# Down projection of the shared experts and the attention's four projections: from float32 matmuls to three single passes of rounded parts and remainders

## The reference

```python
x = x + 0.5 * ffn(layernorm(x))
x = x + attention(layernorm(x))
x = x + 0.5 * ffn(layernorm(x))

def ffn(x):                     # 4096 tokens
    shared = (silu(x @ shared_gate.T) * (x @ shared_up.T)) @ shared_down.T     # 256 -> 512 -> 256
    top_id = argmax(x @ gate_w.T); xs = x * sigmoid(max(x @ gate_w.T))         # 8 experts
    routed = swiglu of xs with the weights of expert top_id                    # 256 -> 512 -> 256
    return shared + routed

def attention(x):               # 16 heads of 16 features, 64 landmarks
    k, q, v = split_heads(x @ Wk), split_heads(x @ Wq) / 4, split_heads(x @ Wv)
    q_l, k_l = means of q and k over each 8 tokens
    s1, s2, s3 = softmax(q k_l'), softmax(q_l k_l'), softmax(q_l k')
    z = pinv(s2)                # 6 iterations, each four 64x64 products in a chain
    return (s1 @ (z @ (s3 @ v))) @ Wo + bo
```

## Time and profile before

| | us |
|---|---|
| median of 3 runs | 1280.99 (1280.19 to 1283.07) |
| the profiled execution | 1283.79 |
| its span, first to last instruction | 1281.9 |
| PE busy | 1176.8 (92%) |
| DVE busy | 708.9 (55%) |
| ACT busy | 559.7 (44%) |
| POOL busy | 539.8 (42%) |

### The profile page before, as it was taken

One profiled execution on the slowest core, in us unless ns is written; L12 is line 12 of the kernel. 1 busy time (PEld: TensorE's weight loads), 2 busy tenths in 40 slices (PEclk: granted clock), 3 DMA queues, 4 the chain that ended last, 5 costly groups with the idle time before them and its releaser, 6 DMA issues.

```text
span 1281.9 us, 28898 instructions
## 1 busy us (share of the span) xinstructions
PE 1176.8 (92%) x10692; PEld 923.2 (72%) x10693; DVE 708.9 (55%) x1387; ACT 559.7 (44%) x887; POOL 539.8 (42%) x603
## 2 busy tenths in 40 slices
PE   4899999999995789999999999986899998999997
PEld 2688877888884456667676676764688887888886
DVE  7533236776663464656757557553642235666664
ACT  2422126666662445445354453421522224666663
POOL 0388205677773122322313231220168503766675
PEclk9899999999998799999999999997799999999999
DMA  8311523222111200000000000000611513222220
GB/s 327 149 50 50 193 77 108 64 68 74 59 61 53 83 2 3 2 3 2 3 2 2 2 2 2 3 2 1 269 44 50 188 37 115 64 65 63 68 70 21
DMA packets 41953, 80.16 MB, mean 63 GB/s; under 512 B 8948, under 2 KB 33655, under 8 KB 40832
## 3 DMA queue, kind: packets, MB, share of 16 engines
q1 hardware_dynamic: 28576, 53.54, 11.5%
q0 software_dynamic: 13280, 25.24, 6.5%
HBM read 57.17 MB, written 27.07 MB: 66 GB/s over the span
## 4 chain that ended last, share of the span: by engine, by line
PE 82%; DVE 11%; issue 4%; ACT 2%; DMA 1%; DVEq 0%; POOL 0%; POOLq 0%; ACTq 0%
PE PS L1396 17%; PE PS L1346 13%; PE PS L1410 10%; PE PS L1355 9%; PE PS L1576 4%; PE PS L1469 4%; PE PS L1589 4%; PE PS L1626 3%; PE PS L1403 3%; PE PS L1477 3%; DVE A_NM L653 2%; DVE A_NM L660 1%; PE PS L1385 1%; PE PS L1536 1%; PE PS L1511 1%
## 5 line engine op out<-in xcount | busy, mean ns | idle before, releaser
L1396 PE MATMUL PS<-WHL,XGH 128*128 128x512 f32 x624 | 217.9, 431 | 8.2 <-DVE XGL L566 4.5
L1228 POOL TENSOR_TENSOR A_A<-A_XC,A_ST 128x320 f32<-128x320 f32 (+1 forms) x96 | 72.9, 774 | 234.3 <-ACT A_ST L1020 234.2
L1410 PE MATMUL PS<-WD,XNT 128*128 x624 | 148.5, 381 | 1.5 <-ACT XNT L956 1.5
L1158 POOL DMA_INDIRECT X<-xs_dram,WHO x78 | 115.0, 1475 | 46.9 <-issue 46.9
L1396 PEld LDWEIGHTS PS<-WHL,XGH 128*128 128x128 f32 x624 | 111.7, 191 | 30.6 <-issue 7.9
L919 ACT ACTIVATE HSB<-PS 128x512 f32<-128x512 f32 x64 | 38.2, 597 | 216.3 <-PE PS L1346 216.3
L1164 POOL DMA_INDIRECT HSB<-shared_dram,WHO x78 | 81.1, 1040 | 114.7 <-DMA shared_dram<-X 91.4
L573 DVE TENSOR_TENSOR XNT<-XNT,PS 128x512 f32<-128x512 f32 x78 | 53.7, 688 | 135.0 <-PE PS L1396 135.0
L514 DVE TENSOR_TENSOR HB<-HSB,PS 128x512 f32<-128x512 f32 x64 | 44.0, 688 | 151.8 <-ACT HSB L919 151.8
L1396 PE MATMUL PS<-WHL,XGL 128*128 128x512 f32 x312 | 124.2, 398 | 0.0
L1410 PEld LDWEIGHTS PS<-WD,XNT 128*128 128x128 f32 x624 | 112.4, 190 | 14.5 <-issue 2.0
(11 more groups left out here) (205 smaller groups left out, 2323.4 us busy)
## 6 DMA issues: line engine op xcount, KB each, us to landing
WG<-in_r_gate SPq DMA_DIRECT2D x2, 4096.0 KB, 15.6
WU<-in_r_up SPq DMA_DIRECT2D x2, 4096.0 KB, 18.0
xs_dram<-X SPq DMA_DIRECT2D x16, 512.0 KB, 2.9
WD<-in_r_down SPq DMA_DIRECT2D x4, 2048.0 KB, 8.3
shared_dram<-X SPq DMA_DIRECT2D x16, 512.0 KB, 8.0
X<-in_x SPq DMA_DIRECT2D x4, 1024.0 KB, 9.2
X<-mid_dram SPq DMA_DIRECT2D x8, 512.0 KB, 3.8
X<-xs_dram,WHO POOLq DMA_INDIRECT x78, 3.4
```

Source lines behind the costliest of these rows:

```text
L1158: pool.indirect_dma_start(out=B["XS"][:, u * D:(u + 1) * D], out_offset=None, in_=xs_dram, in_offset=bass.IndirectOffsetOnAxis(ap=B["WHO"] ...
L1228: pool.tensor_tensor(a, x, st, ALU.add).then_inc(att["a"], 1)
L1396: ins = pe.matmul(banks[bank][:], tok, w[:, k * F:(k + 1) * F], start=(k == 0 and i == 0), stop=(k == KD - 1 and i == 2))
L1410: ins = pe.matmul(banks[7][:, 0:D], B["HT"][:, u * F + f * P:u * F + (f + 1) * P], B["WD"][:, bass.ds(ex * (KF * D) + f * D, D)], start=(f ...
```

## The change

- Shared down projection: SDN is replaced by SDH (rounded, cast by ACT) and SDL (remainder, subtracted by POOL), both float32r. The raw weights are loaded into a free part of WU. SP's load of r_up waits for three splits instead of two.
- The product of the hidden part stays in HSB; ACT copies it to a rounded buffer HHL, DVE subtracts that from it for the remainder. HHL shares HB's memory and has two pairs of buffers.
- PE does three single passes (rounded x rounded, rounded x remainder, remainder x rounded) per token tile and f. Its order is now gate_up n, down n-2 throughout, across group borders. The addition to X (`shared_out`) of group g-1 moves behind f = 1 of group g. The groups are unrolled in all engines.
- Attention: ACT and POOL split WQ, WK, WV and WO at its start. Of the transposed tokens ACT makes the rounded part XTH, DVE the remainder XTL from the same bank (`low_tokens`, two calls per period, after `denominators` and after `s2_shift`). Of the outputs OT, ACT makes OTH after `sums_kept(nxt,1)`, POOL OTL between chain_a 4 and 5. All four projections become three single passes; PE's waits on `xts` become waits on `xtl`.
- Some buffers move (V, NUM onto the raw weights; TT, WS, BSEL into X's spare part), and six semaphores that only DVE waits for become one (`own`).

```diff
-            def shared_group(g, u, first=False, last=False):
+            def shared_out(g):
+                need(dve, "dn", g * KF + KF)
+                need(dve, "xs", g * GT + GT)
+                for jj in range(2):
+                    xg = X[:, g * GT * D + jj * 2 * D:g * GT * D + (jj + 1) * 2 * D]
+                    dve.scalar_tensor_tensor(xg, banks[7 if jj == 0 else 2][:], 0.5, xg, ALU.mult, ALU.add).then_inc(s["x_new"], 1)
+
+            def shared_group(g):
                 for f in range(KF):
+                    hidden = B["HSB"][:, (f % 2) * F:(f % 2 + 1) * F]
                     need(dve, "silu", g * KF + f + 1)
...
+                    dve.tensor_tensor(hidden, hidden, banks[5 + f % 2][:], ALU.mult).then_inc(s["h"], 1)
+                    need(dve, "hh", g * KF + f + 1)
+                    dve.tensor_tensor(B["HHL"][2 * (f % 2) + 1][:], hidden, B["HHL"][2 * (f % 2)][:].bitcast(F32), ALU.subtract).then_inc(s["hl"], 1)
+                    if f == 1 and g > 0:
+                        shared_out(g - 1)
+                    if f == 2 and g < NG - 1:
+                        low_tokens(g + 1, (g + 1) % 2)
...
+            def low_tokens(b, k):
+                dve.wait_ge(att["xth"], count("xth", b, k + 1))
+                part = slice(k * GW, (k + 1) * GW)
+                dve.tensor_tensor(B["XTL"][b % 2][:, part], banks[7 - k][:], B["XTH"][b % 2][:, part].bitcast(F32), ALU.subtract).then_inc(att["xtl"], 1)
...
                 if exists(old):
                     denominators(old)
+                if exists(far):
+                    low_tokens(far, 0)
                 if exists(nxt):
                     s2_shift(nxt)
+                if exists(far):
+                    low_tokens(far, 1)
                 if exists(done):
                     project(done, 0)
...
-                        for high, w in ((SGH, SG), (SUH, SU)):
+                        for high, w in ((SGH, SG), (SUH, SU), (SDH, SD)):
                             act.copy(high[:], w).then_inc(s_split_hi, 1)
...
+                    need(act, "h", g * KF + f + 1)
+                    if g * KF + f >= 2:
+                        need(act, "dn", g * KF + f - 1)
+                    act.copy(B["HHL"][2 * (f % 2)][:], hidden).then_inc(s["hh"], 1)
...
+            def high_outputs(b):
+                for c in range(KD):
+                    act.wait_ge(att["ot"], count("ot", b, c + 1))
+                    act.copy(B["OTH"][:, c * GW:(c + 1) * GW], B["OT"][:, c * GW:(c + 1) * GW]).then_inc(att["oth"], 1)
...
+            def low_outputs(b):
+                for c in range(KD):
+                    part = slice(c * GW, (c + 1) * GW)
+                    wait_alone(att["oth"], count("oth", b, c + 1))
+                    pool.tensor_tensor(B["OTL"][:, part], B["OT"][:, part], B["OTH"][:, part].bitcast(F32), ALU.subtract).then_inc(att["otl"], 1)
...
+            def shared_down(g, f):
+                need(pe, "hl", g * KF + f + 1)
+                if f == 0:
+                    need(pe, "x_new", g * 2)
+                hh, hl = B["HHL"][2 * (f % 2):2 * (f % 2) + 2]
+                part = slice(f * D, (f + 1) * D)
+                for j in range(GT):
+                    to = banks[7 if j < 2 else 2][:, (j % 2) * D:(j % 2 + 1) * D]
+                    for i, (h, w) in enumerate(((hh, SDH), (hh, SDL), (hl, SDH))):
+                        ins = pe.matmul(to, h[:, j * P:(j + 1) * P], w[:, part], start=(f == 0 and i == 0 and j % 2 == 0),
+                                        stop=(f == KF - 1 and i == 2), skip_group_check=True)
+                ins.then_inc(s["dn"], 1)
+
+            for n_f in range(KF * NG + 2):
+                if n_f < KF * NG:
+                    gate_up(n_f // KF, n_f % KF)
+                if n_f == 0:
                     count()
...
+                if n_f >= 2:
+                    shared_down((n_f - 2) // KF, (n_f - 2) % KF)
...
                     for c in range(KD):
-                        ins = pe.matmul(banks[7][:, i * D:(i + 1) * D], B["OT"][:, c * GW + j * P:c * GW + (j + 1) * P],
-                                        WO[:, c * D:(c + 1) * D], start=(c == 0), stop=(c == KD - 1))
+                        for m, (o, w) in enumerate((("OTH", "WOH"), ("OTH", "WOL"), ("OTL", "WOH"))):
+                            ins = pe.matmul(banks[7][:, i * D:(i + 1) * D], B[o][:, c * GW + j * P:c * GW + (j + 1) * P], B[w][:, c * D:(c + 1) * D],
+                                            start=(c == 0 and m == 0), stop=(c == KD - 1 and m == 2))
...
                     pe.wait_ge(att["num"], count("num", old, 2))
-                    pe.wait_ge(att["xts"], count("xts", far, 1))
-                    pe.wait_ge(att["ot"], count("ot", done, 2))
+                    pe.wait_ge(att["xtl"], count("xtl", far, 1))
+                    pe.wait_ge(att["oth"], count("oth", done, 2))
+                    pe.wait_ge(att["otl"], count("otl", done, 2))
                     pe.wait_ge(att["xo"], count("xo", done - 1, 2))
                     project(done, 0)
```

More of the change, by code:

```diff
@@ L178, in ffn_buffers @@
             XHL = [sb(f"XHL{i}_{n}", [P, KD * GW], F32R, shared_with_wd) for i in range(4)]
-        B = dict(WD=b("WD", E * KF * D), WG=b("WG", E * KD * F), WU=b("WU", E * KD * F), HB=b("HB", KF * GW), HSB=b("HSB", 2 * F),
+        B = dict(WD=b("WD", E * KF * D), WG=b("WG", E * KD * F), WU=b("WU", E * KD * F))
+        with ExitStack() as shared_with_hb:
+            HHL = [sb(f"HHL{i}_{n}", [P, GW], F32R, shared_with_hb) for i in range(4)]
+        B.update(HB=b("HB", KF * GW), HSB=b("HSB", 2 * F),
                  OH=b("OH", NT * E),
@@ L226, in emit @@
     fbs = [fb0, fb1]
-    SG, SU = (fb0["WU"][:, i * KD * F:(i + 1) * KD * F] for i in range(2))
+    assert KD * F == KF * D
+    SG, SU, SD = (fb0["WU"][:, i * KD * F:(i + 1) * KD * F] for i in range(3))
     PERIODS = range(-3, NG + 2)
@@ L1122, in ffn_pool @@
             if n == 0:
-                for i, (low, w, high) in enumerate(((SGL, SG, SGH), (SUL, SU, SUH))):
+                for i, (low, w, high) in enumerate(((SGL, SG, SGH), (SUL, SU, SUH), (SDL, SD, SDH))):
                     pool.wait_ge(s_split_hi, i + 1)
@@ L1249, in attention_pool @@
                 chain_a(b, 3)
+                if b == PERIODS[0]:
+                    for i in range(1, 4):
+                        low_weights(i)
                 chain_a(b, 4)
+                if exists(old):
+                    low_outputs(old)
                 chain_a(b, 5)
@@ L1371, in ffn_tensor, with gate_up @@
-            shared_group(0, 0, first=True)
-            shared_group(1, 1)
-            with pe.Fori(1, NG // 2) as i:
-                for u in range(2):
-                    shared_group(i * 2 + u, u)
+                pe.wait_ge(s_split_lo, 3)
+            def gate_up(g, f):
+                if f == 0:
+                    need(pe, "xl", g + 1)
+                need(pe, "h", max(g * KF + f - 1, 0))
+                xh, xl = B["XHL"][2 * (g % 2):2 * (g % 2) + 2]
+                for bank, high, low in ((f % 2, SGH, SGL), (5 + f % 2, SUH, SUL)):
+                    for k in range(KD):
+                        part = slice(k * F + f * P, k * F + (f + 1) * P)
+                        for i, (w, tok) in enumerate(((high, xh), (high, xl), (low, xh))):
+                            ins = pe.matmul(banks[bank][:], w[:, part], tok[:, k * GW:(k + 1) * GW],
+                                            start=(k == 0 and i == 0), stop=(k == KD - 1 and i == 2))
+                ins.then_inc(s["gu"], 1)
@@ L1467, in project_qk @@
                 i, c = divmod(n, KD)
+                high, low = ((B["WQH"], B["WQL"]), (B["WKH"], B["WKL"]))[i]
+                th, tl = B["XTH"][b % 2], B["XTL"][b % 2]
                 for k in range(KD):
-                    ins = pe.matmul(banks[7 if n == 0 else 6][:], (WQ, WK)[i][:, k * D + c * P:k * D + (c + 1) * P],
-                                    B["XTS"][b % 2][:, k * GW:(k + 1) * GW], start=(k == 0), stop=(k == KD - 1))
+                    for m, (w, tok) in enumerate(((high, th), (high, tl), (low, th))):
+                        ins = pe.matmul(banks[7 if n == 0 else 6][:], w[:, k * D + c * P:k * D + (c + 1) * P], tok[:, k * GW:(k + 1) * GW],
+                                        start=(k == 0 and m == 0), stop=(k == KD - 1 and m == 2))
                 ins.then_inc(att["qk_ready"], 1)
```

167 lines of the change are left out of this document (71 added, 96 removed).

## The result

| | before | after |
|---|---|---|
| median, us | 1282.59 (1280.19 to 1284.93, 5 runs) | 1272.44 (1269.82 to 1274.35, 5 runs) |
| ratio | | 0.9926 [0.9908, 0.9945] |
| the profiled execution | 1283.79 | 1274.35 |
| its span | 1281.9 | 1272.2 |

The kernel became faster by 10.2 us, a little less than half of the 20.7 forecast; the time lies inside the range. First the page of the kernel after: PE's busy time, PE's clock in 40 slices, the chain by engine.

The account below looks back on a forecast made before the run. TensorE, busy 92% of the span, was taken to bound the kernel. Shared experts -12.8 and attention -7.9 gave -20.7 us from 1283.8, so 1263.1, and a median of 1260.3, 2.8 lower; range 1247 to 1276.

Parts of the forecast that it names:

- 0.120 us per pass: Down, V and output blocks: a rounded 256-column pass takes 0.120 us, expected 0.110 to 0.130, its weight load overlapped.
- rival "slower": Down, V and output blocks: weight load and stream don't overlap; 1304 at 0.16 us a pass, about 1370 at 0.22; chance 0.08.
- Shared experts, -12.8: Both feed-forwards: 2 x (-9.4 + 0.6 + 1.0 + 0.9) + 1.0 = -12.8 us net.
- the first group's 1.0: First group of each shared stage: DVE's queue with the router's steps delays the tokens PE needs, +1.0 us.
- the last group's 0.9: Last group of each shared stage: its update queues behind weight casts and subtractions and ends late for PE, +0.9 us.
- The residual update without margin: Shared stage: the update, moved behind the next group's second remainder, costs 0.1 us for six groups, 0.6 in all.
- rival "larger waits": Residual update and attention: 0.5 us more each loses 7 us in 14 groups, 4 in eight periods; 1271; chance 0.18.
- A new wait of 1.61 ahead of the output block in four periods: Attention, b = 2 to 5: the output block writing bank 7 waits 1.61 us for DVE's low part, queued behind the reciprocal.
- Full periods at 54.6: Attention periods b = 2 to 5, with both batches: each takes 54.6 instead of 55.0 us.
- -1.16 - 1.08 + 1.81 = -0.4: Each attention period with both batches: shorter projection blocks against new waits for low parts, net -0.4 us.
- three more half-clock slices: Edges of the attention: less PE work may add half-clock slices, some 1.7 us each, taken as inside the range.
- The end, +0.6: End of attention: the last outputs' split adds 2.3 us, two shorter blocks at 1.2 GHz save 1.7, net +0.6.

Follow-up runs that it names:

- filled kernel: The full change plus eleven unread 128x256 passes while TensorE waits ahead of the output block, periods b = 2 to 5; 1265.53 us, 0.9859 of before.
- wait-alone kernel: Shared experts alone, plus one TensorE wait on DVE's first s2_shift reduction ahead of the output block, b = 2 to 5; 1281.74 us, 1.0 of before.
- shared experts alone: The kernel before with only the change's feed-forward lines, attention left in float32; 1272.65 us, 0.9924 of before.
- own bank: The full change, but in periods b = 2 to 5 the first output block writes bank 0 instead of bank 7, DVE's order matched; 1265.89 us, 0.9862 of before.
- reordered: The full change with the second chain product and second token turn moved ahead of the first output block, no instruction added; 1274.09 us, 0.9931 of before.

## Why the prediction was right or wrong

- **0.120 us per pass: right.** Measured 120 ns, within the bounds of 110 to 130. This was the number that the sign hung on. The rule of the Trainium skill that would have made it 0.22 (TensorE: Matmul & The Clock Gate, section The mechanism, overlap only when the row group differs) isn't borne out: the loads here are on all 128 rows and hidden. The same section of the Trainium skill also says that TensorE pulls a load ahead when it targets the background weight buffer; by that the loads can be hidden, and the 120 ns agree with it. The rival "slower" is out.
- **Shared experts, -12.8: about right, 1 to 2 us too much.** Alone they gave 0.9924 [0.9899, 0.995], which is -9.7 [-13.0, -6.4]. In the profiled executions the attention's first turn comes 5.5 earlier (forecast for the first feed-forward: -9.4 + 0.6 + 1.0 + 0.9 + 1.0 = -5.9), and the second shared stage gains 5.5 (forecast 6.9), from -2.2 at its start to -7.7 behind it. The other 2.0 up to the -9.7 at the end arise in the routed stage, which the change doesn't touch; they are not explained. Term by term: the first group's 1.0 was 0.6 and 0.8; the last group's 0.9 was 0.6 and 0.3, where before had waited 0.55 and 0.3 as well, so nothing was added. The residual update without margin, taken at 0.1 a group, cost more: a group takes 16.99 us, while four blocks of 4.18 would be 16.72, so 0.27 each. The list of waits doesn't show it, since most of them lie under the end of the matmul record before, but the timeline does: PE's block starts 0.43 behind the last gate/up pass, where 0.23 is the distance of passes, and 0.15 behind the end of the update (87.73 + 1.28).

```profile
87.73 1.28 DVE L527 SCALAR_TENSOR_TENSOR X<-PS,X 128x512 f32<-128x512 f32 x2
...
88.73 0.39 PE L1398 MATMUL PS<-XHL,SUL 128*128 128x512 f32 x1
...
89.16 0.36 PE L1411 MATMUL PS<-SDH,HHL 128*128 128x256 f32 x1
```

  The rival "larger waits" (0.5 more in 14 groups, 7 us) was right on the place and not on the size.
- **Down-to-down distance of 4.16: right.** The block ahead of the one shown starts at 63.20, 4.18 earlier: 12 passes of 0.120 and 2.74 of gate/up, which the change leaves as it was.
- **A new wait of 1.61 ahead of the output block in four periods: right** (1.48 four times, 5.9 in all), by the walk through DVE's queue. PE's wait for A_TM rose from 4.8 to 6.9: the gain of the fourth Q/K block went there, as the prediction has it.
- **Full periods at 54.6: wrong, and this is the step that failed.** They took 55.9 to 57.1. The step "-1.16 - 1.08 + 1.81 = -0.4" priced the wait at its length. The filled kernel, in which the wait is as long and the clock stays up, has 54.6, 54.7, 54.6 and 54.3, so the sum stood as a whole; the term for the clock was missing. I had it at the edges of the attention only and called it inside the range ("three more half-clock slices"); its price of 1.7 each was right (the wait-alone kernel: 3.2 less 1.5), their number and place weren't: six more of 3.4 us within the four periods, and the four periods took 226.1 - 218.4 = 7.7 more than forecast (part of the low stretches lies in waits that are there anyway).
- **The early periods:** b = -2 gained 0.4 (forecast 1.2), b = -1 2.3 (1.2), b = 0 0.8 (1.3), b = 1 0.1 (0.9; 3.4 us at 1.2 GHz fall into it). Together 3.6 against 4.6.
- **b = 6, 7, 8: right.** -1.1, -0.5, -0.6 against -1.2, -0.5, -0.6.
- **The end, +0.6: right in kind, 0.5 too low.** The wait rose from 3.80 to 6.52 (2.7; forecast 2.3), and the two blocks became shorter; from -4.8 the offset comes to -3.7 at the first transposes behind, so +1.1. Then 1.7 went by the clock at the second logits (a stretch of 1.2 GHz at 913 us that before doesn't have).
- **The sum:** attention forecast -7.9, measured in the trace +1.8 between the turn at 413 and the end; alone 1.0005. Off by 9.7, of which 8.1 in b = 2 to 5.

What stays open: what exactly decides whether the clock falls. Shown is that the attention's change lowers it (every run), that filling the new wait with 11 full passes brings it back (every run), and that a wait of this length alone went with a fall in four periods of four (one execution). Shown too is that the clock can fall without it: with the same instructions and pauses in b = 1 (wait alone against shared experts alone), with the wait taken away (own bank, reordered), and with a few full passes (5). No experiment shifts a period in time without changing its work, so the rival that the fall depends on where the stretch meets the program, besides the pauses, is untested.

The fastest versions are the filled kernel (1265.5) and the one with its own bank (1265.9), both 1.4% below before and, by the ratios, 0.7% below the change as it was made. The bank kernel adds no work, and I would keep it, though its times spread more (1263.1 to 1268.2, the filled kernel 1264.2 to 1265.6) and its clock still falls in three of the four periods.

## What to carry to other kernels

Price a new wait on TensorE twice: its length, and what the granted clock does behind it, above all where another pause and only small (32- or 64-row) matmuls stand next to it, as here. In the profile, look for passes of one form at two distances (0.120 and 0.213 here) before explaining a loss by anything else. If a wait can't be moved, large matmuls without a use in it can be worth more than they cost, but try the number of them: 11 saved 7 us here, and 5 nothing. And look at the granted clock of every run before trusting a difference seen in one profile.

## What the runs showed of the hardware

- TensorE's clock fell to 1.2 GHz after pauses of 1.3 and 1.5 us with 0.67 us of 32-row matmuls between, in stretches of 3.4 us; in the kernel with the wait alone each cost 1.7. The Trainium skill (TensorE: Matmul & The Clock Gate, section A second HAM failure mode: psum-queue depth-cycling) tells of short pauses between groups of matmuls that let the clock swing between its two levels; this case's traces agree (after: 0.95 between 560 and 780 us, with stretches at 1.2 GHz in each period), and show besides that filling the pause with 11 unused passes ended it there (1.00).
- In the reordered kernel the clock fell while PE was busy with 64x64 matmuls (1.70 for a chain product in place of 1.32), 1.7 us behind the end of a pause of 1.29. With the same instructions and pauses it fell in one execution and not in another (period b = 1, 1.76 and 1.32).
- A rounded pass of 256 columns on 128x128 weights takes 0.120 us, its weight load hidden; a float32 one, 0.43. Three rounded passes are thus 0.36, 17% less than one float32 matmul, where Q/K passes of 512 columns (0.227 to 0.230) give 0.68 to 0.69 against 0.86, 20% less.
- DVE's subtraction for the remainder of the hidden part (`L535`, both inputs in SBUF) took 0.69 in 54 of 64 cases, as the product of the same size; the other ten took 0.72 to 1.53, each beside work of GpSimd and the six longest (1.06 to 1.53) beside its copy of X (`L1171`). In the reordered kernel one took 1.90. The product (`L533`, one input in PSUM) never took more than 0.69.
